# A two-layer gated kernel on one Trainium2 core: 26 idle TensorE instructions in six places of the mixer and the tail are left out

## The reference, cut to what matters

```python
x = x + tanh(g_xattn[0]) * L0_xattn(ctx, ctx, layernorm(x), ssm_kernel, D, 8)   # the mixer
x = x + tanh(g_ffn[0])   * L0_ffn(layernorm(x), gate_w, mask_up_w, gate_proj_w, up_proj_w, down_proj_w, inv_map)
x = x + tanh(g_xattn[1]) * L1_xattn(layernorm(x), ctx, mask)
x = x + tanh(g_ffn[1])   * L1_ffn(layernorm(x), ternarize(w_fc), ternarize(w_proj))
```

## Time and profile before

| | before |
|---|---|
| median of 3 runs | 231.15 us (230.76 to 231.24) |
| the profiled execution's own time | 230.63 us |
| its span, first to last instruction | 228.9 us |
| mean granted TensorE clock | 0.989 |
| TensorE busy | 217.5 us, 1405 instructions |
| VectorE busy | 177.5 us |
| ScalarE busy | 111.2 us |
| GpSimd busy | 77.7 us |

### The profile page before, as it was taken

How to read it: one execution, slowest core, us unless ns; L and a number is a source line. 1 busy time by engine, 2 the same in 40 slices (tenths; PEclk the granted TensorE clock), 3 DMA queues, 4 the chain that set the end, 5 groups by cost and what they waited for, 6 DMA issues and landing times.

```text
span 228.9 us, 4229 instructions
## 1 busy us (share of the span) xinstructions
PE 217.5 (95%) x1405; PEld 198.7 (87%) x1405; DVE 177.5 (78%) x507; ACT 111.2 (49%) x221; POOL 77.7 (34%) x113
## 2 busy tenths in 40 slices
PE   7679899999999999999999999999999999998994
PEld 7579899998889889889889898889989988998883
DVE  4289999988989978698986597873587638846874
ACT  2341367942355343746353573494932682435443
POOL 2279998376553321010130343200101211201530
PEclk9799999999999999999999999999999999999998
DMA  5699953000000007000000000000000100001011
GB/s 170 138 292 345 325 172 111 3 0 3 0 1 3 0 0 229 3 1 0 3 0 0 3 0 0 3 3 0 0 3 0 46 0 3 0 6 44 0 47 46
DMA packets 14068, 11.46 MB, mean 50 GB/s; under 512 B 2944, under 2 KB 13792, under 8 KB 14048
## 3 DMA queue, kind: packets, MB, share of 16 engines
q1 hardware_dynamic: 11792, 11.03, 15.7%
q10 hardware_dynamic: 2256, 0.18, 0.7%
HBM read 10.14 MB, written 1.07 MB: 49 GB/s over the span
## 4 chain that ended last, share of the span: by engine, by line
PE 76%; DMA 8%; DVE 8%; ACT 2%; POOL 2%; issue 2%; ACTq 0%; SPq 0%; DVEq 0%; POOLq 0%
PE bank L808 25%; PE bank L646 12%; PE bank L838 6%; PE bank L812 4%; PE bank L873 4%; PE bank L889 4%; PE bank L836 3%; PE bank L693 3%; DMA ctx<-in_ctx_rows 3%; PE bank L694 3%; PE bank L695 3%; DMA lag_rows<-lags 2%; PE bank L639 2%; DMA toe<-lag_rows 2%; PE bank L725 1%
## 5 line engine op out<-in xcount | busy, mean ns | idle before, releaser
L808 PE MATMUL bank<-w_split,xt 128*128 128x512 f32 (+1 forms) x288 | 66.3, 378 | 0.0
L808 PEld LDWEIGHTS bank<-w_split,xt 128*128 128x128 f32 x288 | 51.5, 188 | 7.0 <-issue 0.2
L1352 DVE SCALAR_TENSOR_TENSOR act<-silu,scal,bank 128x176 f32<-128x176 f32 (+2 forms) x80 | 23.7, 355 | 17.1 <-ACT silu L1044 17.1
L1044 ACT ACTIVATE silu<-bank 128x512 f32<-128x512 f32 (+1 forms) x24 | 13.5, 563 | 28.8 <-PE bank L812 28.7
L838 PE MATMUL bank<-d_split,a_t 128*128 128x512 f32 x70 | 24.9, 396 | 0.0
L1513 POOL TENSOR_TENSOR fold<-prod 128x512 f32<-128x512 f32 x16 | 20.7, 1296 | 11.6 <-DVE att L1211 7.6
L898 ACT ACTIVATE a_t<-bank 128x512 fp32r<-128x512 f32 (+1 forms) x24 | 13.4, 559 | 19.8 <-PE bank L646 16.4
L561 POOL TENSOR_TENSOR kv<-ctx_ext 128x640 f32<-128x640 f32 x15 | 19.5, 1306 | 9.7 <-ACT ctx_ext L898 4.0
L836 PE MATMUL bank<-d_split,a_t 128*128 128x256 f32 x77 | 20.5, 281 | 0.0
L1454 POOL TENSOR_SCALAR ve<-mv 128x2 f32<-128x2 f32 (+2 forms) x11 | 3.1, 280 | 49.6 <-DVE mv L1134 49.6
L1099 DVE TENSOR_TENSOR a_t<-bank,a_t 128x512 fp32r<-128x512 f32 (+1 forms) x24 | 15.3, 639 | 3.5 <-ACT a_t L898 3.5
(11 more groups left out here) (162 smaller groups left out, 466.3 us busy)
## 6 DMA issues: line engine op xcount, KB each, us to landing
toe<-lag_rows SPq DMA_DIRECT2D x3, 512.0 KB, 7.5
ring<-in_down_p SPq DMA_DIRECT2D x2, 704.0 KB, 5.0
ctx<-in_ctx_rows SPq DMA_DIRECT2D x2, 512.0 KB, 6.7
ring<-in_gate_p SPq DMA_DIRECT2D x2, 512.0 KB, 7.1
ring<-in_up_p SPq DMA_DIRECT2D x2, 512.0 KB, 5.9
out_x<-x_res SPq DMA_DIRECT2D x3, 256.0 KB, 2.1
tern_w<-in_w_fc SPq DMA_DIRECT2D x1, 640.0 KB, 4.4
tern_w<-in_w_proj SPq DMA_DIRECT2D x1, 640.0 KB, 5.6
```

The costliest lines, as they stand in the source:

```text
L808: pe.matmul(psum((name, b, c))[:, 0:w_cols], lhs, w_split[:, w, kt, part, cols], start=i == 0, stop=False)
L1044: drain(act_e.activation(silu[:, n % 2, 0:w_cols], psum(("gate", b, c))[:, 0:w_cols], ACT.Silu), ("gate", b, c))
L1352: drain(dve.scalar_tensor_tensor(out=act[:, whole], in0=silu[:, n % 2, here], scalar=scal[:, b, g:g + 1], in1=psum(("up", b, c))[:, here], ...
```

## The change

The list of the six counts and the list of their places are made empty. The branch that issues them stays and is no longer reached; no other step moves against another.

```diff
@@ -66,7 +66,7 @@
 WARMS = [12, 0, 0]
-KEEPS = [2, 1, 4, 2, 3, 1]
+KEEPS = []
@@ -90,7 +90,7 @@
     "downs": [170, 184, 203, 224, 240, 259, 279, 296],
-    "keeps": [74, 81, 106, 109, 110, 322],
+    "keeps": [],
     "router0": [89, 92, 104, 108, 112, 119, 120, 121, 131],
```

## The result

Without the 26 instructions the kernel takes 234.27 us, the median of 4 runs (233.66 to 236.02), against 230.95 us (230.48 to 231.24, also 4 runs) before: a ratio of 1.0178, 95% interval 1.0132 to 1.0223. It is slower by 3.3 us. The way was forecast, the size was not: 232.4 us was predicted and the range ended at 233.1.

The account below looks back on a forecast made before the run. TensorE was busiest, but waits behind all six places hid the removed work (gain 0). A clock fall added 1.3 us: 230.63 + 0 + 1.3 = 231.9, or 231.15 + 1.3 = 232.4 from the median; range 230.8 to 233.1.

Parts of the forecast that it names:

- places 4 and 5: Ten idle instructions at 48.90 us, before three convolutions: gain 0, as the turn of rt waits for VectorE's chain.
- a rival, for the faster side: Convolutions and GpSimd's kv come 1.1 us earlier without places 4 and 5: up to 1.1 us faster, chance 0.11.
- The clock: Term for a 3.4 us half-clock stretch starting between 53.4 and 55.5 us: 1.3 us lost, bounds 0 and 1.7.
- The place itself: Stretch from 50.8 to 54.2 us, thin in TensorE weight loads: 1.29 us of loads left instead of 2.33.
- the forecast pause: TensorE's wait before the turn of rt, about 52.8 us: grows from 0.34 to about 1.45 us.
- the forecast fall: Granted clock drops to 0.50 in the middle for about 3.4 us: chance 0.52, 1.3 us lost.
- Places 1, 2, 3 and 6: Sixteen idle instructions at 37.0, 39.05, 46.81 and 219.56 us: gain 0, since TensorE waits for ScalarE or VectorE behind them.
- the clock did not hold: Rival that the full clock holds throughout the middle, leaving only zero gains: 231.15 us, chance 0.32.
- the saved slots: Rival that earlier convolutions and kv products at places 4 and 5 count: up to 1.1 us, 230.0 us, chance 0.11.
- the tail kept its clock: Rival that the clock falls near 220 us without place 6: 1.5 us more, 232.7 us, chance 0.05.
- a second low stretch in the tail: Tail rival's case with clock falls in both middle and tail: 234.0 us, outside the range; tail rival's chance 0.05.

Follow-up runs that it names:

- e3: Kernel before, with places 4 and 5 moved behind the three convolutions and 9 products there instead of 5: 232.20 us against 230.48, ratio 1.0100.
- e6: Changed kernel, with GpSimd's two collided kv products put behind the fold that waits for VectorE's drains: 232.06 us against 230.46 before, ratio 1.0059.
- e9: As e6, with 5 idle products (10 instructions) added behind the three convolutions: 229.1 to 233.5 us, ratio to before 1.0006.
- e2: Kernel before, with places 1, 2, 3 and 6 left out and places 4 and 5 kept: 230.32 us, ratio 0.9991.
- e4: Kernel before, with places 4 and 5 replaced by a TensorE wait for VectorE's write of line 1292: 230.69 us against 230.48, ratio 1.0024.
- e13: Kernel before without places 1, 2, 3, 6; one down-weights turn in place 3, one GpSimd kv product moved later: 230.06 us against 230.38, ratio 0.9987.

## Why the prediction was wrong

**The step that failed** is the one on places 4 and 5. I wrote that GpSimd's next kv product "comes 1.1 us earlier, but its fold waits for VectorE's drains, which stand behind the same chain. Gain: 0". The first half came true (1.01 us). But I asked only who waits for that product, not what runs beside it. VectorE's chain, on which I let the turn of rt depend, was taken as fixed; it became 1.6 us longer, 6.43 us instead of 4.82. I had even made the earlier kv products a rival, for the faster side. The price of this, 1.6 us, was in no term of the sum and not in the upper bound, and it is half of the loss that the profile shows. e3 has it with the clock as before in eight of 12 runs (1.4 us), and in e6, where the two kv products are out of the way, the cast and line 1300 are back at 0.19 and 0.29 us and the chain at 4.78.

The trace of before held the warning: line 1300 at 51.23 and the kv product at 51.25. The Trainium skill, "SBUF — State Buffer", section "Who interferes with whom", says that a VectorE instruction with two inputs in SBUF, or a cast or copy in its two-port mode, and a GpSimd instruction that reads SBUF exclude each other, and whichever starts first makes the other wait to its end. By that rule these runs come out as they did: the cast (1.13 us), line 1300 (1.00), 1308 (0.99, 0.87), 1340 (1.40) each end 0.05 to 0.28 us behind a kv product that had begun first, and the MAX8 of line 1303, which has one input, took 0.36 us in the kernel before, under a running kv product. No row shows in which mode the cast ran.

**The clock:** a fall came, and the term was mis-sized. Taken at 1.3 us, it measured 1.67 in the trace of the change and about 2 between the two groups of e3. I had let the pause hide a little of the low stretch; but that stretch began at 56.6, behind the pause, and fell wholly on work of TensorE. The place itself was judged well as to its kind (1.24 us of loads in 3.4, forecast 1.29), partly by luck, since the collision made the pause 3.07 us instead of 1.45. (By the prediction's own rows its convolutions cover 0.58 us of the stretch and not 0.65, which makes 1.22.) e6, without that collision, shows that the forecast pause can be enough, with a low stretch in its profile behind 1.42 us; but only two of its 12 runs had two low stretches, while the mean clocks of the change's four leave room for two in each. So the forecast fall may have become so frequent only by the longer pause that the collision made; that is argued and not shown. The one pair that differs in the pause alone, e6 and e9, had two and one such runs of 12. And the low stretch began at 56.6 us, behind the 53 to 56 us that I had named, by about the 1.6 us of the collision.

**Places 1, 2, 3 and 6** were right at 0: e2. The logits' load moved by 0.1 us and waited 1.29 us (forecast 1.2). That no more than one fall of the clock in the middle could be lost, and so the top of the range, was wrong.

**The rivals:** the clock did not hold; the saved slots did not count; in the profile the tail kept its clock until behind its last product. The collision was none of them. One rival did name nearly the time that was measured, 234.0 us against 234.27, by a second low stretch in the tail. The profile has none there; the two longest executions had one more somewhere, so for them a part of that rival stays open.

## What to carry to other kernels

An idle instruction on one engine can be a spacer for others: before leaving it out, move everything behind it forward on paper, on every engine, and look at what then runs at the same time, not only at who waits for whom. For VectorE and GpSimd this means listing the casts and two-input operations on the path and the GpSimd products that would slide over them. Where a spacer is needed, a wait did as well as ten products as far as the times tell (e4). Real work in place 3, with the ten products kept and one kv product moved, gave the shortest stretch (e13), but no time that can be told from the kernel before.

## What the runs showed of the hardware

- A stretch of TensorE work may be followed by the half clock without any long pause: 1.02 us was the longest in e3_behind between 40 us and its fall, 1.42 us in e6_kv_late. Each low stretch inside lasted 3.4 us, and in the change the clock came back at 60.0 us while TensorE did turning instructions alone (57.0 to 60.3 us).
- GpSimd also waits for VectorE: where line 1300 began 0.02 us ahead, the kv product took 1.38 us instead of 1.25. In every meeting seen here the one that began second paid: 0.1 us on GpSimd, which nobody waited for, where line 1300 was 0.02 us ahead, and 0.7 us on the path where it was behind.
- Profiled executions differ by up to 3.1 us in when the logits' load starts, with nearly the same work ahead of it (46.4 us in e9, which has no low stretch ahead of it and none of the six places, and 49.5 in e4), which hides effects of 0.3 us in the times; read from one load to another within a profile, the stretches of two kernels agree to 0.04 us where nothing differs.
